# Attention scores on 64 rows of TensorE, two heads side by side, in a two-block transformer kernel

## The reference

```python
x = L0_attn_x                                    # (16, 512, 128), 16 heads of 8 channels
q, k, v = jnp.split(jnp.einsum('btc,fc->btf', _layernorm(x), W_attn), 3, axis=-1)
scores = jnp.einsum('bhqd,bhkd->bhqk', q, k) * scale
bias = slopes[:, None, None] * rel[None, :, :]
bias = jnp.where(causal[None, :, :], bias, -jnp.inf)
att = jax.nn.softmax(scores + bias[None], axis=-1)
y = jnp.einsum('bhqk,bhkd->bhqd', att, v)        # heads joined, projected by W_proj, added to x
```

## Time and profile before

| | |
|---|---|
| median of 3 runs | 1864.93 us (1862.35 to 1865.44) |
| profiled execution | 1872.14 us, span 1870.4 us |
| TensorE matmul busy | 1385.0 us (74%) |
| VectorE busy | 1232.8 us (66%) |
| ScalarE busy | 793.6 us (42%) |
| GpSimd busy | 819.3 us (44%) |
| mean granted clock of TensorE | 0.857 |

### The profile page before, as it was taken

The page is one execution under the profiler, slowest core; times in us unless marked ns, Lnnn a source line. Parts: engine busy times, 40 slices in busy tenths (PEclk is TensorE's granted clock), DMA queues, the critical chain, the costliest instruction groups (busy, mean ns, idle before and its releaser), DMA issues. The chain is left out here.

```text
span 1870.4 us, 34099 instructions
## 1 busy us (share of the span) xinstructions
PE 1385.0 (74%) x9402; PEld 856.1 (46%) x9403; DVE 1232.8 (66%) x3656; ACT 793.6 (42%) x1625; POOL 819.3 (44%) x719
## 2 busy tenths in 40 slices
PE   1788988989888889975911726662639999999996
PEld 0344544444444445534801613332616555565554
DVE  4676776767667667655765228986776666666663
ACT  0254554555445445550120326663514444444443
POOL 3222222222222112003401537986428888888886
PEclk9899999999999999995555866655559999999999
DMA  3433333233223223414501430020133333333332
GB/s 77 138 75 69 75 74 73 64 68 74 66 67 74 55 60 83 82 51 164 189 4 44 89 64 29 28 109 6 67 125 43 42 41 42 42 42 42 41 42 35
DMA packets 72747, 124.17 MB, mean 66 GB/s; under 512 B 17776, under 2 KB 42160, under 8 KB 70240
## 3 DMA queue, kind: packets, MB, share of 16 engines
q0 software_dynamic: 38656, 59.35, 20.0%
q1 hardware_dynamic: 26000, 51.17, 8.1%
q10 hardware_dynamic: 8032, 12.93, 1.9%
HBM read 65.19 MB, written 57.68 MB: 66 GB/s over the span
## 5 line engine op out<-in xcount | busy, mean ns | idle before, releaser
L428 DVE TENSOR_REDUCE mx<-psS 128x1 f32<-128x384 f32 (+3 forms) x704 | 429.4, 638 | 196.8 <-PE psS L322 185.3
L489 ACT ACTIVATE probs<-psE 128x1024 f32<-128x1024 f32 (+2 forms) x384 | 328.3, 884 | 300.6 <-PE psE L338 298.3
L1902 POOL DMA_INDIRECT out<-ex_y,ex_idx x144 | 236.1, 1639 | 48.3 <-issue 42.7
L322 PE MATMUL psS<-kop,qop 96*128 96x128 bf16 (+3 forms) x1024 | 247.2, 306 | 0.0
L338 PE MATMUL psE<-qop,kop 128*128 128x512 bf16 (+3 forms) x1024 | 229.2, 305 | 0.0
L319 PE MATMUL psS<-maskq,identb 128*128 128x128 bf16 (+2 forms) x704 | 177.1, 252 | 52.7 <-DMA kop<-qkv_scr 24.6
L335 PE MATMUL psE<-maskk,identb 128*128 128x128 bf16 (+2 forms) x704 | 174.3, 248 | 45.4 <-DMA qop<-mT 42.9
L252 POOL TENSOR_TENSOR rstd<-veps,mhalf 128x4 f32<-128x4 f32 x16 | 16.6, 1037 | 386.0 <-DVE veps L377 386.0
L347 PE MATMUL psY<-probs,vaug 128*32 128x512 f32 (+3 forms) x2048 | 173.4, 449 | 0.0
L1893 POOL DMA_INDIRECT ex_xg<-expert_tab,ex_idx x144 | 142.8, 991 | 66.0 <-issue 42.1
L1876 DVE SCALAR_TENSOR_TENSOR ex_h<-ex_psG,ex_w,ex_up 128x352 f32<-128x352 f32 x144 | 84.0, 584 | 109.6 <-PE ex_psG L1943 100.4
(11 more groups left out here) (319 smaller groups left out, 2628.2 us busy)
## 6 DMA issues: line engine op xcount, KB each, us to landing
y_scr<-ysb SPq DMA_DIRECT2D x64, 256.0 KB, 2.1
qkv_scr<-parts POOLq DMA_DIRECT2D x32, 384.0 KB, 3.1
qop<-qkv_scr POOLq DMA_DIRECT2D x16, 384.0 KB, 6.9
kop<-qkv_scr POOLq DMA_DIRECT2D x16, 384.0 KB, 9.5
expert_tab<-table_rows SPq DMA_DIRECT2D x1, 4352.0 KB, 13.5
qop<-qkv_scr POOLq DMA_DIRECT2D x16, 256.0 KB, 7.1
kop<-qkv_scr POOLq DMA_DIRECT2D x16, 256.0 KB, 11.8
pj_num<-y_scr SPq DMA_DIRECT2D x16, 256.0 KB
```

The source lines that it names most:

```text
L322: mm = pe.matmul(out[:, h, :], qop[n][0:96, hh, P * j:P * j + P], kop[n][0:96, hh, 0:w], start=False, stop=(h == nh - 1), skip_group_check ...
L428: dve.tensor_reduce(mx[:, j, h0:h0 + nh], psS[u % 2][:, 0:nh * w].rearrange("p (h k) -> p h k", h=nh), AX, ALU.max).then_inc(s_su, 1)
L489: act.activation(dst, src, ACT.Exp).then_inc(s_ex, 1)
L1902: pool.indirect_dma_start(out, bass.IndirectOffsetOnAxis(ap=idx[t % 8][:], axis=0), y[m][:], None, compute_op=ALU.add).then_inc(s_sc[m], 16)
```

## The change

S and E use 64 rows. `qop` and `kop` hold 8 heads in partitions 0-63 and the other 8 in 64-127; a unit has a half `p`, and units come in pairs, one for each half, so that consecutive matmuls read different row halves and write different banks. `psS` and `psE` become rings of three single banks with 12 units each. The mask matmul of E goes. In its place a ladder of ten constant rows (`COARSE`) subtracts 1e30 from pairs of key and query that lie in different pieces of 48, the later piece on the key's side, which keeps the exponential small; the exact triangle is cut afterwards on `probs` by GpSimd, `affine_select` on a 128 x 4 x 128 block for each key tile (`clear_future`). V waits for these selects (`s_msk`) instead of the exponentials. S keeps its mask matmul. VectorE's four memsets go, as every row is written. The statistics are taken in step 3, two batches ahead, and the transposes come first in step 0. `place` is cut in `place_q` and `place_k`, twelve DMAs of half the size, and GpSimd's stream places them, the splits and `factors` between the selects. Columns of the weights are reordered to match. The core of the diff:

```diff
+HALF = P // 2
+HH = H // 2
+COARSE = 48
+NCOARSE = (T - 1) // COARSE
 ROW_ALIBI = 8 * len(TERMS)
-ROW_MAX = 96
+ROW_COARSE = ROW_ALIBI + 3
+ROW_MAX = ROW_COARSE + NCOARSE
+ROW_END = ROW_MAX + 2
...
-        psS = [ctx.enter_context(nc.psum_tensor(f"psS{i}", [P, T], F32)) for i in range(2)]
-        psE = [ctx.enter_context(nc.psum_tensor(f"psE{i}", [P, 2, T], F32)) for i in range(2)]
+        psS = [ctx.enter_context(nc.psum_tensor(f"psS{i}", [P, T], F32)) for i in range(3)]
+        psE = [ctx.enter_context(nc.psum_tensor(f"psE{i}", [P, T], F32)) for i in range(3)]
...
-        UN = 11
-        EN = 6
-        s_units = []
-        for j in range(TT):
-            n = [4, 2, 1, 1][j]
-            s_units += [(j, h, n) for h in range(0, HG, n)]
-        e_units = [(0, 0, 2), (0, 2, 2), (1, 0, 2), (1, 2, 2), (2, 0, 4), (3, 0, 4)]
-
-        ORDER = ["S0", "S1", "E0", "M", "V2", "V3", "E1", "S2", "S3", "E2", "S4", "E3", "S5", "S6", "E4", "S7",
-                 "E5", "S8", "V0", "V1", "S9", "S10"]
+        UN = 12
+        EN = 12
+
+
+        s_units = [(j, p, h, 2 if j < 2 else 1) for j in range(TT) for h in ((0,) if j < 2 else (0, 1)) for p in range(2)]
+        e_units = [(j, p, h, 1 if j < 2 else 2) for j in range(TT) for h in ((0, 1) if j < 2 else (0,)) for p in range(2)]
+        E_PAST = (4, 8, 10, 12)
+
+        ORDER = ["S0", "E0", "M", "V2", "S1", "E1", "V3", "S2", "E2", "S3", "E3", "V0", "S4", "E4", "S5", "E5", "V1"]
         REST = 16 * (nb // 2 - 1)
...
-                    for a in range(2):
-                        sp.dma_start(qop[m][ROW_MAX + a:ROW_MAX + a + 1, HG * g:HG * g + HG, :], mT[HG * a:HG * a + HG])\
+                    for p in range(2):
+                        sp.dma_start(qop[m][HALF * p + ROW_MAX:HALF * p + ROW_END, 2 * g:2 * g + 2, :], mT[HG * p:HG * p + HG])\
...
+                pool.wait_ge(s_pw, 32 * b + 16)
+                for row, k in ROWS:
+                    for p in range(2):
+                        q_src = qkv_scr[n, 0, 0:k].rearrange("a (d c h) q -> c (a d) (h q)", d=D, c=2)[p]
+                        lo = HALF * p + row
+                        pool.dma_start(qop[n][lo:lo + 8 * k].rearrange("p h q -> p (h q)"), q_src).then_inc(s_op, 16)
+
+            def place_k(n, b):
                 pool.wait_ge(s_pw, 32 * b + 32)
-                for row, k in rows:
-                    k_src = qkv_scr[n, 1, 3 - k].rearrange("(d h) q -> d (h q)", d=D)
-                    pool.dma_start(kop[n][row:row + 8 * k].rearrange("p h q -> p (h q)"), k_src.unsqueeze(0).to_broadcast([k, D, H * T]))\
-                        .then_inc(s_op, 16)
...
+                    pool.affine_select(diag, diag, [[0, HG], [1, P]], ALU.is_ge, 0.0, base=0, channel_multiplier=-1).then_inc(s_msk, 1)
...
+                    if st == 1 and more:
+                        split_rest(b + 1, 1)
+                    if st == 2 and more:
+                        place_q(1 - b % 2, b + 1)
+                    if st == 3 and b + 2 < nb:
+                        factors(b + 2)
+                    clear_future(u, 0)
+                    if st == 0 and more:
+                        split_rest(b + 1, 0)
+                    if st == 2 and more:
+                        place_k(1 - b % 2, b + 1)
+                    for j in range(1, TT):
+                        clear_future(u, j)
...
+                    if st == 0 and not last:
+                        x_transposes(b + 1, use_next(b, 0))
                     for what in ORDER:
-                        if what == "S4" and st == 0 and not last:
-                            x_transposes(b + 1, use_next(b, 0))
-                        if what == "S7" and st == 0 and not last:
+                        if what == "S3" and st == 0 and not last:
                             project(0, use_next(b, 1))
+                        if what == "S5" and st == 0 and not last:
+                            project(1, use_next(b, 2))
+                        if what == "S4" and st == 2 and not last:
+                            project(2, use_next(b, 3))
...
+                            both = []
+                            for u in (2 * k, 2 * k + 1):
+                                j, p, h0, nh = s_units[u]
+                                w = P * (j + 1)
+                                out = psS[u % 3][:, 0:nh * w].rearrange("p (h k) -> p h k", h=nh)
+                                both.append((j, p, h0, w, out))
+                                if not isinstance(b, int) or UN * G * b + UN * g + u > 2:
+                                    pe.wait_ge(s_su, UN * G * b + UN * g + u - 1)
+                                pe.matmul(out[:, :, P * j:w], identb[:], maskq[:, 0:nh, :], start=True, stop=False, skip_group_check=True)
                             for h in range(nh):
-                                hh = HG * g + h0 + h
-                                mm = pe.matmul(out[:, h, :], qop[n][0:96, hh, P * j:P * j + P], kop[n][0:96, hh, 0:w],
-                                               start=False, stop=(h == nh - 1), skip_group_check=True)
-                            mm.then_inc(s_sr, 1)
+                                for j, p, h0, w, out in both:
+                                    hh = 2 * g + h0 + h
+                                    mm = pe.matmul(out[:, h, :], half(qop[n], p, ROW_MAX)[:, hh, P * j:P * j + P],
+                                                   half(kop[n], p, ROW_MAX)[:, hh, 0:w],
+                                                   start=False, stop=(h == nh - 1), skip_group_check=True)
+                                    if h == nh - 1:
+                                        mm.then_inc(s_sr, 1)
...
-                            pe.wait_ge(s_ex, EN * u_exp + u)
-                            for h in range(0, nh, per):
-                                out = bank[:, h // per, 0:per * W[j]].rearrange("p (h q) -> p h q", h=per)
...
-                                    hh = HG * e + h0 + h + a
-                                    mm = pe.matmul(out[:, a, :], kop[m][:, hh, P * j:P * j + P], qop[m][:, hh, P * j:T],
...
+
+                            for h in range(e_units[2 * k][3]):
+                                for u in (2 * k, 2 * k + 1):
+                                    j, p, h0, nh = e_units[u]
+                                    if h == 0 and (not isinstance(b, int) or EN * u_exp + u > 2):
+                                        pe.wait_ge(s_ex, EN * u_exp + u - 1)
+                                    hh = 2 * e + h0 + h
+                                    mm = pe.matmul(psE[u % 3][:, W[j] * h:W[j] * h + W[j]],
+                                                   half(kop[m], p, ROW_END)[:, hh, P * j:P * j + P],
+                                                   half(qop[m], p, ROW_END)[:, hh, P * j:T],
+                                                   start=(h == 0), stop=(h == nh - 1), skip_group_check=True)
+                                    if h == nh - 1:
+                                        mm.then_inc(s_er, 1)
...
-                            pe.wait_ge(s_ex, 1 + EN * u_v + [2, 4, 5, 6][k])
+                            pe.wait_ge(s_msk, TT * u_v + k + 1)
...
-                    if not last and st == 0:
-                        project(1, use_next(b, 2))
-                    if not last and st == 2:
-                        project(2, use_next(b, 3))
...
-            dve.memset(qop[0][:].bitcast(F32), 0.0).then_inc(s_init[0], 1)
-            dve.memset(kop[0][:].bitcast(F32), 0.0).then_inc(s_init[0], 1)
...
-            dve.memset(qop[1][:].bitcast(F32), 0.0).then_inc(s_init[1], 1)
-            dve.memset(kop[1][:].bitcast(F32), 0.0).then_inc(s_init[1], 1)
+            norm_stats(1)
+            norm_apply(1, 1)
...
-                if st == 0 and not last:
-                    if n == 1:
-                        dve.wait_ge(s_rest, REST)
-                    norm_stats(b + 1)
+                ahead = st == G - 1 and (not isinstance(b, int) or b + 2 < nb)
+                if ahead:
+                    dve.wait_ge(s_rest, REST)
+                    norm_stats(b + 2)
+                if st == 1 and not last:
+                    split(b + 1, 1)
...
+                    if k == 6 and ahead:
+                        norm_apply(b + 2, use_next(b, 0) + 1)
...
-                    if k == 8 and st == 0 and not last:
+                    if k == 7 and st == 0 and not last:
                         split(b + 1, 0)
-                    if k == 0 and st == 1 and not last:
-                        split(b + 1, 1)
...
+                ahead = st == 0 and not last
+                if ahead:
+                    copy_x(use_next(b, 0))
...
+                        act.activation(probs[st % 2][j][:, 2 * p + h0:2 * p + h0 + nh, :].rearrange("p h q -> p (h q)"),
+                                       psE[k % 3][:, 0:nh * W[j]], ACT.Exp).then_inc(s_ex, 1)
+                        if k == 3 and there(u - 1):
```

(28 more changed lines are left out.)

158 lines of the change are left out of this document (73 added, 85 removed).

## The result

The changed kernel takes 1784.6 us against 1865.2 (medians): a ratio of 0.956, 95% interval 0.952 to 0.959, so 81 us less where 40 were forecast, and 0.4 us below the foot of the range. The profiled execution took 1782.7 us (span 1781.0) against 1872.1: 89.4 us between the two traces. Some executions of a kernel are slower than its others by 1.5% or more, and the profiled ones of e1, e3, e10 and e11 are such; the ratios leave them out and the medians don't, so where it matters the times of the others are given too.

A forecast was written before the change was run, and what follows sets the result against it. TensorE's in-order chain was taken as the bound, VectorE starved behind two score banks. Per batch 44.2 + 0.7 (DMA) + 1.5 (clock) = 46.4 against 48.8 us; with batch 15, start and tail 1832, as median 1825; range 1785 to 1910.

The forecast's parts named there:

- the stall behind V0: In each four-head step, VectorE free at 5.7 us waits for S4, queued behind V0, until 6.55: 0.85 us.
- the select: GpSimd's diagonal-tile operation, four a step, for which no row had a price: taken as 1.0 us, bounds 0.5 to 2.2.
- steps 2 and 3: Last two four-head groups of a batch, with q issues and v projection, then the moved statistics: 10.3 and 10.8 us.
- the DMA term: TensorE's wait for the maxima's transfer behind the k placements, 2.9 us mean before: 0.7 us a batch kept, bounds 0 and 4.
- the start: Before the first scores: two memsets gone and the first placement issued in smaller shares, 4 us gained in all.
- the tail: End of the attention: the last two steps get a select on their path, 1.5 us lost.
- The clock term: TensorE's granted clock falls behind the 3.5 us hole at a batch's beginning: 1.5 us a batch charged.
- Plain step: One group of four heads without preparation of the next batch, summed: 9.4 us against 10.3.
- (d): Rival: score pairs don't run side by side; 2.1 us more TensorE work a step, about 1.3 showing: 1905 us, chance 0.05.
- rival (c): TensorE idle a quarter of each step, so its clock falls in four steps of ten: 85 us more, 1910; chance 0.13.
- Steps 0 and 1: First two four-head groups of a batch, where V1 and V0 wait for selects behind GpSimd's splits: 12.9 and 10.2 us.
- rival (a): Selects cheap at 0.6 us each and clock holds: 2.7 us a batch less, 1787 us; chance 0.12.

The follow-up runs named there:

- e1: Changed kernel with both score matmuls of a pair reading the first half's rows, so pairs run in series: 2023.9 us.
- e3: Changed kernel with the select of tile 1 moved ahead of the split of q's rest on GpSimd, at a batch's first step: 1755.6 us.
- e10: Changed kernel with the second eight heads' placement transfers sent to rows 0 to 47 of a spare tile: 1812.4 us.
- e11: e3 with the first of the two GpSimd operations of each split given to ScalarE: 1756.3 us.
- e7: Changed kernel without the GpSimd selects, V waiting for the exponentials themselves: 1730.8 us.
- e9: Changed kernel with its twelve placement transfers issued together behind the last select of their step, instead of six and six: 1873.7 us.
- e8: Changed kernel with a full-height matmul of zeros put back on TensorE ahead of each E pair, beside the selects: 1846.6 us.
- e12: Changed kernel with V2 behind S1 and V0 behind S4 in TensorE's order, and without GpSimd selects: 1774.7 us (two executions).
- e4: Changed kernel with V2 behind S1 and V0 behind S4 in TensorE's written order: 1836.6 us.

## Why the prediction was right or wrong

What bounds, the order of events and the sign were right. What failed is the size of the terms in the sum: a batch came to 46.4 us on paper and 43.2 on the chip. Too dear were VectorE's work and the stall behind V0 in every step, the select, steps 2 and 3, the DMA term and the start; too cheap was the tail. The clock term was about right.

- *Plain step*: 9.4 forecast, 8.73 measured. VectorE's own work was 7.6, not 7.9, because back-to-back reductions take less than the mean of single ones that I summed (six in 3.45 us); the stall behind M, V2 and S1 was 0.45 (forecast 0.4, right), the one behind V0 0.68 (0.85), the small one none. Batch 15 gave 6.2 us for my 3.5.
- *Switches and pairs*: full concurrency was right, and so was 0.1 us a switch. Where I priced its loss (d) at 1.3 us a step, 1905, the direct cost was 0.97 in a plain step and less elsewhere, and the clock added far more.
- *TensorE's work*: 6.9 us a step forecast; in the plain step it is busy for 7.8 of 8.73. (The 9.3 for the kernel before doesn't follow from its own terms either: 6.0 + 0.4 + 2.3 = 8.7; the trace has it busy for 9.6 of 10.27.) So TensorE is idle for a tenth of a step and not a quarter, on which rival (c) was built.
- *Steps 0 and 1*: 23.1 forecast without a clock charge, 22.7 measured with 1.3 of it inside, so 21.4; hole, place and cause as written, and e7 and e3 prove the cause. The select itself was 0.64, not 1.0: I had taken a value between memset's 0.53 and 1.64, and it lies near the former. *Steps 2 and 3*: 10.3 and 10.8 against 9.8 and 10.2.
- *DMA*: 0.7 us a batch kept, none measured. I had argued with the timing; e9 shows that the spacing within step 2 isn't it, e10 that it is, at least in part, which partitions the rows go to. No row of before could show this.
- *Clock*: 1.5 us a batch charged for the stretch behind the hole. It came in each of 14 batches, and e8 prices it at 1.3. Another 43.2 - 42.7 = 0.5 is the mean's distance from the batch shown, most of it the one disturbed batch. Rival (c) didn't come: the mean is 0.94. Its own arithmetic was off as well, 2 x 5.3 + 1.6 is 12.2 and not 12.7, which makes it 1897. The Trainium skill, "TensorE: Matmul & The Clock Gate", section "HAM oscillation — how this bites in real kernels", has a kernel that falls to half clock at each of its waits, which are longer than those here. The trace shows the same behind a hole of 2.85 us, once a batch; the 0.70 of e1 is not of that kind, for there TensorE filled its steps.
- *Start and tail*: 7.6 gained for 4 (the first scores start at 42.10, not 50.19), 2.7 lost for 1.5.

Sum: of the 3.2 us a batch, steps 0 and 1 are 1.7, steps 2 and 3 1.1, DMA 0.7, less 0.3 for the clock. Over 14 batches 3.2 is 44 us, with 2.7 (batch 15) and 3.6 (start) and less 1.2 (tail): the 49 us that are missing between 40 and 89. The result is that of rival (a), 1787, to which I gave 0.12, but it had one of its two conditions, a select of 0.6; the other, no clock charge, wasn't met. That its number fits is luck: it kept my plain step, DMA and start, and what these were too dear made up for the clock. I had centred each unknown term between its bounds and added the cautious values up.

## What to carry to other kernels

Where several unknown prices stand in one sum, work out what it gives when all come out at their low end together, and let the range hold it. A part alone says little of a change: pairs without the third bank lose all, and halved transfers without the new rows lose too. An engine that serves two masters needs its order read instruction by instruction: one select moved ahead of one split gave 29 us, twelve DMA issues in front of one select cost 89, and filler work belongs ahead of the matmul that has to wait (about 25 us in e12).

## What the runs showed of the hardware

- VectorE's small operations from one on-chip tile to another are held up by a GpSimd select beside them, until it ends: 0.174 to 0.176 us in all 64 casts of e7, without selects, 0.54 to 0.61 in the plain steps of e4 and e8, where they overlap. The Trainium skill, "SBUF — State Buffer", section "Who interferes with whom", has both: casts can take the port pair that is shared with GpSimd under an exclusive lock, operations with two inputs in that memory contend for it with a GpSimd operation that reads there, and reductions never do. The trace agrees on the reductions: 597 ns in the mean with and without selects.
- The software queue's transfers took 36% more DMA engine time with the rows placed in partitions 0 to 47 alone than in 0 to 47 and 64 to 111 (29.3 to 21.6%, e10 and the changed kernel).
- The granted clock fell behind a TensorE wait of 2.85 us in 14 of 14 batches of the changed kernel and behind one of 1.7 us in eight of 14 in e8, where the stretch at half clock cost 1.3 us.
- It fell furthest where TensorE had most to do, in e1 (mean 0.70 in the trace, with TensorE busy in all of 18.74 us at 0.50), and not in the kernel with more idle time (0.94). Why is open.
- An idle head of 3 to 5 us on TensorE at the start of a batch, with more packets on the queue named instruction in the same traces (60 to 62 against 17), makes the step some 6 us longer (16.8 for 10.9 us in e12). That this queue is the cause isn't shown.
